# Upper half of the keys from x alone, by weights multiplied on the chip, from the second chunk on

## The reference

```
ct_kv = x @ Wd_kv_w + Wd_kv_b                         # latent, 128 numbers for each token
kt_c  = heads(ct_kv @ Wu_k_w + Wu_k_b)
kt_r  = heads(_rope(x @ Wk_r_w + Wk_r_b, cos, sin))
key   = kt_c + kt_r                                   # 16 heads of 16 numbers
value = heads(ct_kv @ Wu_v_w + Wu_v_b)
```

## Time and profile before

| What | Value |
|---|---|
| Runs | 1925.49, 1926.04, 1926.55 us |
| Profiled execution, its own time | 1926.29 us |
| Its span, first to last instruction | 1924.5 us |
| Mean granted TensorE clock | 0.987 |
| TensorE busy | 1849.6 us (96%) |
| ScalarE busy | 1802.0 us (94%) |
| VectorE busy | 1580.2 us (82%) |
| GpSimd busy | 173.7 us (9%) |
| First exponential of the attention stage | at about 126 us |

### The profile page before, as it was taken

How to read it: one execution, slowest core, us unless ns; L and a number is a source line. 1 busy time by engine, 2 the same in 40 slices (tenths; PEclk the granted TensorE clock), 3 DMA queues, 4 the chain that set the end, 5 groups by cost and what they waited for, 6 DMA issues and landing times.

```text
span 1924.5 us, 31443 instructions
## 1 busy us (share of the span) xinstructions
PE 1849.6 (96%) x12996; PEld 449.9 (23%) x12996; DVE 1580.2 (82%) x1499; ACT 1802.0 (94%) x2022; POOL 173.7 (9%) x132
## 2 busy tenths in 40 slices
PE   8989999999999999999999999999999999999975
PEld 3432222122222222222222222222222222222234
DVE  4858888888888888888888888888889888988467
ACT  3479999999999999999999999999999999999946
POOL 5735400000000000000000000000000000500010
PEclk9989999999999999999999999999999999999987
DMA  4453111111110111111121001111121101111002
GB/s 142 153 172 116 18 21 26 26 26 26 26 26 20 18 18 22 26 26 26 25 70 26 22 17 18 22 26 25 26 48 26 26 19 19 18 23 26 1 24 88
DMA packets 161367, 73.41 MB, mean 38 GB/s; under 512 B 129952, under 2 KB 146592, under 8 KB 160736
## 3 DMA queue, kind: packets, MB, share of 16 engines
q1 hardware_dynamic: 158272, 66.85, 15.0%
q10 hardware_dynamic: 2944, 4.47, 0.8%
HBM read 49.13 MB, written 20.84 MB: 36 GB/s over the span
## 4 chain that ended last, share of the span: by engine, by line
ACT 54%; PE 31%; issue 9%; DVE 4%; DMA 1%; POOL 0%; SPq 0%; ACTq 0%; DVEq 0%; POOLq 0%
ACT arena L901 54%; PE PS L704 15%; PE PS L655 9%; PE PS L1179 4%; PE PS L744 1%; DVE arena L961 1%; PE PS L1328 1%; DMA arena<-tables_dram 1%; DVE bn L832 1%; DVE arena L937 0%; DMA w<-weights_dram 0%; DVE absmax L1771 0%; DVE arena L1805 0%; DVE arena L824 0%; ACT arena L864 0%
## 5 line engine op out<-in xcount | busy, mean ns | idle before, releaser
L901 ACT ACTIVATE arena<-PS 128x1024 f32<-128x1024 f32 x1860 | 1707.8, 1325 | 8.3 <-PE PS L655 5.0
L704 PE MATMUL PS<-arena,Vh 128*32 128x512 f32 x8192 | 1092.6, 606 | 4.1 <-DVE arena L961 4.1
L655 PE MATMUL PS<-Qst,Kst 49*128 49x512 f16 x4096 | 724.0, 384 | 24.5 <-ACT arena L901 4.3
L961 DVE SCALAR_TENSOR_TENSOR arena<-arena 128x2048 f32<-128x2048 f32 x282 | 646.0, 2291 | 0.1
L937 DVE TENSOR_SCALAR arena<-PS 128x512 int32<-128x512 f32 x376 | 259.4, 690 | 247.1 <-PE PS L655 243.3
L655 PEld LDWEIGHTS PS<-Qst,Kst 49*128 49x128 f16 x4096 | 187.7, 93 | 1039.3 <-ACT arena L901 1008.8
L704 PEld LDWEIGHTS PS<-arena,Vh 128*32 128x32 f32 x8192 | 161.3, 108 | 317.5 <-issue 302.5
L957 DVE SCALAR_TENSOR_TENSOR arena<-arena 128x2048 f32<-128x2048 f32 x94 | 216.4, 2302 | 0.0
L945 DVE TENSOR_SCALAR arena<-arena 128x2048 int32<-128x2048 int32 x94 | 116.2, 1236 | 8.5 <-DVE arena L961 0.5
L947 DVE TENSOR_SCALAR arena<-arena 128x2048 int32<-128x2048 int32 x94 | 116.8, 1242 | 0.0
L1496 POOL TENSOR_SCALAR nmr<-mv 128x16 f32<-128x16 f32 x1 | 0.3, 262 | 1256.7 <-DVE mv L1660 1256.7
(11 more groups left out here) (118 smaller groups left out, 480.1 us busy)
## 6 DMA issues: line engine op xcount, KB each, us to landing
Kst<-k_halves SPq DMA_DIRECT2D x64, 128.0 KB
Qst<-q_halves SPq DMA_DIRECT2D x64, 128.0 KB
Vh<-head_values SPq DMA_DIRECT2D x30, 256.0 KB, 5.5
k_halves<-parts_or_sums SPq DMA_DIRECT2D x16, 256.0 KB, 2.9
q_halves<-parts_or_sums SPq DMA_DIRECT2D x16, 256.0 KB, 2.8
Kst<-k_halves SPq DMA_DIRECT2D x64, 64.0 KB
Qst<-q_halves SPq DMA_DIRECT2D x64, 64.0 KB
head_values<-arena SPq DMA_DIRECT2D x1, 4096.0 KB, 16.4
```

The source lines that it names most:

```text
L655: return nc.tensor.matmul(out, Kst[par][low:low + HK + 1, at:at + 128], Qst[par][low:low + HK + 1, j * CH:(j + 1) * CH], start=True, stop= ...
L704: last = nc.tensor.matmul(bank(value_bank(t))[32 * j:32 * j + 32, :], Vh[t % 2][:, kt, :], moving, start=kt == first, stop=kt == last_kt)
L901: nc.scalar.activation(ring(at, k), bank(g % SLOTS * SLOT, k), ACT.Exp, scale=EXP_SCALE).then_inc(a.exp, 1)
L961: last = nc.vector.scalar_tensor_tensor(out=t, in0=t, scalar=POLY[3 - j], in1=power if j == 3 else mantissa, op0=ALU.add, op1=ALU.mult)
```

## The change

It forms the product of the latent weights with the upper key weights once, `Wd_kv_w @ Wu_k_w[:, 128:]`, adds the upper half of `Wk_r_w`, and from chunk 1 on takes the upper keys as two products of x with these weights; the latent bias goes through the same weights into a bias of its own. Chunk 0 stays as it was, three products. The weights lie where the values are written later, and the small products use bank 4, which chunk 1's `KHI` uses next.

TensorE turns the two halves of the latent weights by two transposes ahead of chunk 1's `DKV`, ScalarE copies them to SBUF, and ahead of chunk 1's `DQ_` TensorE makes two products of 128 columns and one of a single column. VectorE adds the rest ahead of its first addition.

```diff
+UPPER_BEFORE = "add", 0, "k"
...
+        latent_t = arena[:, 22 * K1:22 * K1 + D]
+        upper_w = arena[:, 22 * K1 + D:22 * K1 + 2 * D].rearrange("p (k n) -> p k n", k=2)
+        upper_bias = small[:, 0:1]
+        UPPER_BANK = PRODUCT_BANK["p", 1, KHI]
...
-                    KHI: ([wcut(W_KR, k, D, 128) for k in range(2)] + [wcut(W_UK, lo=128)], x2 + [kv]),
+                    KHI: ([upper_w[:, k, :] for k in range(2)], x2) if c else
+                         ([wcut(W_KR, k, D, 128) for k in range(2)] + [wcut(W_UK, lo=128)], x2 + [kv]),
...
-                if e in (UK_, KHI):
+                if e == KHI and c:
+                    pe.wait_ge(s_upper_w, 2)
+                elif e in (UK_, KHI):
                     pe.wait_ge(s_w2, 16)
                     pe.wait_ge(s_ev, DONE["p", c, DKV])
...
+            def turn_latent_weights():
+                pe.wait_ge(s_const, 1)
+                pe.wait_ge(s_ev, DONE[BANK_BEFORE["p", 1, KHI]])
+                for k in range(2):
+                    last = nc.tensor.transpose(PS[:, UPPER_BANK * CH + k * 128:UPPER_BANK * CH + (k + 1) * 128],
+                                               wcut(W_DKV, k, DQ), ident[:, :])
+                last.then_inc(s_upper, 1)
+
+            def upper_weights():
+                pe.wait_ge(s_upper_t, 1)
+                at = UPPER_BANK * CH
+                for k in range(2):
+                    nc.tensor.matmul(PS[:, at + D + k * 128:at + D + (k + 1) * 128], latent_t[:, k * 128:(k + 1) * 128],
+                                     wcut(W_UK, lo=128), start=True, stop=True)
+                nc.tensor.matmul(PS[:, at:at + 1], wcut(W_UK, lo=128), bias[:, B_DKV:B_DKV + 1],
+                                 start=True, stop=True).then_inc(s_upper, 1)
+
             for p in PRODUCTS:
+                if p == ("p", 1, DKV):
+                    turn_latent_weights()
+                if p == ("p", 1, DQ_):
+                    upper_weights()
...
+                if p == ("p", 1, DKV):
+                    act.wait_ge(s_upper, 1)
+                    nc.scalar.copy(latent_t, PS[:, UPPER_BANK * CH:UPPER_BANK * CH + D]).then_inc(s_upper_t, 1)
+                if p == ("p", 1, KHI):
+                    act.wait_ge(s_upper_w, 2)
...
+            def upper_weights():
+
+                dve.wait_ge(s_upper, 2)
+                at = UPPER_BANK * CH
+                past = w[:, W_KR:W_UK].rearrange("p (k n) -> p k n", k=2)[:, :, 128:256]
+                nc.vector.tensor_tensor(upper_w, PS[:, at + D:at + 2 * D].rearrange("p (k n) -> p k n", k=2), past,
+                                        ALU.add).then_inc(s_upper_w, 1)
+                nc.vector.scalar_tensor_tensor(out=upper_bias, in0=PS[:, at:at + 1], scalar=K_SCALE, in1=bias1[:, 0:1],
+                                               op0=ALU.mult, op1=ALU.add).then_inc(s_upper_w, 1)
+
+            dve.wait_ge(s_bias, 2)
             for name, c, n in STEP:
+                if (name, c, n) == UPPER_BEFORE:
+                    upper_weights()
```

More of the change, by code:

```diff
@@ L468, in build @@
         s_swap = {n: [sem(f"{n}_swapped{p}") for p in range(2)] for n in "kq"}
+        s_upper = sem("upper_key_products")
+        s_upper_t = sem("latent_weights_turned")
+        s_upper_w = sem("upper_key_weights_made")
         s_rope = sem("rope_products")
@@ L1365, in evacuate @@
                 at = {DKV: bias[:, B_DKV:B_DKV + 1], DQ_: bias[:, B_DQ:B_DQ + 1], KR_: bias[:, B_KR:B_KR + 1],
-                      UK_: bias[:, B_UK:B_UK + 1], KHI: bias1[:, 0:1], QR_: bias[:, B_QR:B_QR + 1],
+                      UK_: bias[:, B_UK:B_UK + 1], KHI: upper_bias if c else bias1[:, 0:1], QR_: bias[:, B_QR:B_QR + 1],
                       UQ_: bias[:, B_UQ:B_UQ + 1], QHI: bias1[:, 1:2]}[e]
```

## The result

The changed kernel takes 1929.0 us, the median of twenty runs (1926.8 to 1929.9). The kernel before takes 1925.6 on the same chip, also of twenty (1923.8 to 1928.2). The ratio is 1.0016, with a 95% interval of 1.0010 to 1.0023. So the change costs 3.4 us between the medians (3.1 by the ratio, 1.9 to 4.4 by its interval). The forecast was 1929.2, or +3.3 on the profiled execution. The profiled execution of the changed kernel took 1928.93 against 1926.29, and its first exponential of the attention stage starts at 129.43 against 126.28: 3.15 us later, 2.6 us of which are left at the end.

The account below looks back on a forecast made before the run. VectorE and GpSimd taking turns at shared ports were taken to bound the projection stage. 0.8 (late chunk 7 addition) + 3.3 (collision) - 0.8 (slack) gave +3.3 us, about 1929.2 us; range 1925.0 to 1931.2.

Parts of the forecast that it names:

- What bounds the stage: Projection stage: VectorE, full from 39.4 to 76 us through taking turns with GpSimd at shared ports, sets the pace.
- Removed: TensorE, upper key groups from chunk 1 on: seven fp32 products of 512 columns go, saving 6.0 us.
- Added on TensorE: Before chunk 1's first and second groups: eight records of transposes and small products, 1.6 us, bounds 0.9 and 3.4.
- VectorE's added steps and their cover: Before VectorE's first addition: 256-column addition (0.40) and one-column step (0.2), hidden in its wait for GpSimd until 26.23.
- The head shift: Head of VectorE's queue: later turned keys of chunk 1 delay the addition at 39.45 by 0.5 us, ends 0 and 1.7.
- Chunk 7's first addition: VectorE, chunk 7's keys: the addition starts 0.8 us late, from the 0.5 plus what chunk 6's keys add.
- The collision: VectorE's four steps on chunk 7's keys each wait a GpSimd turn of 0.95: 3.8 less 0.5 for pauses, 3.3 us.
- TensorE's lead: TensorE near chunk 7: of 4.3 us of lead, 2.1 remain behind x's load, 3.0 after chunk 7's upper keys.
- The landing: Last table load before the first exponentials: lands 10.66 us after its issue, left unchanged.
- The collision does not form: Rival at chunk 7's keys: swaps land late or VectorE locks first; -1.4 to +1.5 us, middle 1926.3; chance 0.30.
- TensorE sets the end: Rival for the projection stage: VectorE's queue follows TensorE, stage ends 4.3 us early, 1921.8; chance 0.07.
- The head shift passes whole: Rival at VectorE's queue head: shift 1.7 instead of 0.5, plus the collision, 1930.6 to 1931.6; chance 0.15.

Follow-up runs that it names:

- e9: Changed kernel with GpSimd's three turning steps for each part moved to VectorE, ahead of its addition; 1919.82 us against 1926.07 before, ratio 0.9971.
- e10: Kernel before the change with the same move of GpSimd's turning steps to VectorE as e9; 1923.97 us against 1926.07 before, ratio 0.9991.
- e4: Changed kernel with SyncE's last table load issued ahead of the eight loads of the first head's stack; 1927.51 us, ratio to before 1.0011.
- e1: Changed kernel with a third product put back into each upper-key group from chunk 1 on, set-up kept; 1926.49 us, ratio to before 1.0011.
- e3: Changed kernel with GpSimd waiting to begin chunk 6's queries until VectorE has made chunk 7's key low part; 1925.97 us, ratio to before 1.0006.
- e5: Changed kernel with GpSimd held ahead of chunk 6's queries only until VectorE's cast of chunk 7's keys; 1927.79 us, ratio to before 1.0000.
- e6: Changed kernel with e3's wait, last table load between halves of the first head's loads, key lengths and shifts moved into the values; 1926.95 us, ratio 0.9997.
- e8: Changed kernel with e3's wait and the last table load between the two halves of the first head's loads; 1926.89 us, ratio to before 0.9994.
- e2: Kernel before the change with the latent part of the upper keys of chunks 1 to 7 left out, nothing added; 1929.28 us, ratio 1.0021.
- e7: Kernel before the change with all the edits of e6, as its control; 1928.41 us, ratio to before 1.0002.

## Why the prediction was right

The mechanism is the one predicted: the saving closes GpSimd's pause, VectorE's last key steps wait their turns, and the key store holds the reload. That 1929.0 lies so near 1929.2 is luck in part: two terms below came out by errors that cancel.

**What bounds the stage.** Right. VectorE is full from 39.4 us on in both kernels and runs the same 24 instructions. e9 and e10 show it from the other side.

**Removed.** Seven products, 6.0 us: the groups are two records shorter and chunk 7 begins 3.3 us earlier on TensorE.

**Added on TensorE.** Mis-sized. The eight records cost 0.9 us, the lower bound, where I took 1.6 by the weight load of 190 ns. The trace does show 190 ns for each weight load of the small products, but they overlap one another: four take 0.52 us together, and one starts every 0.11 us (21.81, 22.25 after four, 22.47 after two more). That pace is what the records cost. The turned keys of chunk 1 were 0.6 us late by the clock of the trace, and 1.05 against TensorE's own start: in this execution chunk 0's first latent product began at 13.81, before at 14.26.

**VectorE's added steps and their cover.** Right: 0.42 and 0.15, in the idleness that ended at 26.2 before. The second addition now starts at 25.93.

**The head shift.** Too large, though inside its ends of 0 and 1.7. The addition of 39.45 came at 39.16, which is +0.2 if those 0.45 us of an earlier start are taken off. Predicted was +0.5. The sign that I gave, a first addition some 0.5 us later, did not show.

**Chunk 7's first addition.** +0.8 predicted, +0.72 measured (93.45), by other parts than I gave. Chunk 6's addition came 0.44 early (85.70; before 86.14), and from there to chunk 7's two turns more than before were met where I had one: the addition of 85.70 took 1.67 and the cast behind it 1.57, 0.98 and 0.88 more. The sum, -0.44 + 0.98 + 0.88 - 0.62 of idleness used up, is 0.80. A start too early and a turn too many cancel; the agreement is luck.

**The collision.** Right in place and size: the low part's end at 100.13 for 100.15, the reload of the tables at 103.17 for 103.1. This term carries the forecast. One of its parts was wrong: I took four full turns less 0.5 us of pauses between dependent steps. The pauses are as long as before (0.1 us from the addition's end to the cast, in both traces), and the first turn was a half: the four steps are longer by 0.45, 0.88, 0.94 and 1.06, together 3.33 for 3.3. So the addition took 1.14 and not the 1.64 that I had named as a sign.

**TensorE's lead.** Wrong in its cause, and 2.1 us where 3.3 were measured. Gaps were predicted near 78, ahead of chunk 7, for x. The gap came ahead of 74.30, inside chunk 6, for another reason: the latent keys' evacuation stood behind one that waited 3.62 us for VectorE (rows at 72.31 on ScalarE and 74.30 on TensorE). x was there in time. I also had chunk 7's turned keys at 81.8, measured 80.64, and chunk 6's queries at 87.7, measured 86.53; both only fill GpSimd's queue sooner. (The evacuation at 90.68 is that of chunk 6's turned queries, not of the upper ones, as the prediction once calls it.) The 8.2 us gap ahead of 98.07 I hadn't named. It is off the chain in the changed kernel, and e4 shows it is second.

**The landing.** Left at 10.66, measured 11.05: +0.4, which the steps behind it gave back.

**The rivals.** "The collision does not form" would have left 0.69 and 1.22 in those rows; e1 and e3 are what it looks like. "TensorE sets the end" needed a VectorE that isn't held by GpSimd; in e9 and e10 it isn't, and there the gain is 4.2 us. That I gave it 4.3 is luck: my 4.3 holds the mis-sized 1.6 for the set-up, and with the measured 0.9 it would be 5.1. "The head shift passes whole" falls with the 39.16.

Two slips of the pen in the sums change nothing: 96.08 + 4.1 is 100.18, and 1926.04 + 3.3 is 1929.3.

Open: from the first exponential to the last instruction takes 1797.5 to 1800.6 us in these executions, in kernels with the same attention stage. Why it varies by 3 us isn't known. A shift of 1 us or so is blurred by it, so e3, e5, e6 and e8 can't be ranked by their times.

## What to carry to other kernels

Where VectorE and GpSimd are both near full in a stretch, add up VectorE's steps at their lengths when alone, and for each GpSimd step what it holds VectorE up. From 39.4 to 76 us before, VectorE's 24 steps alone would take 6 times 3.29 (0.69, 0.69, 0.69 and 1.22), 19.7 us; the other 16.9 of the 36.6 fall on 18 GpSimd steps, an estimate of 0.94 for each. Where this sum is the bound, work taken from a third engine gains little, and loses where it closes a pause of GpSimd's in which VectorE's last steps on the path ran alone. Look for VectorE durations of two kinds for one shape (0.69 and 1.64), with its reductions from PSUM unchanged. What helped here was to take GpSimd out and not to move its steps in time: a step of 32 rows costs VectorE less to do (0.67) than to be held by (0.94 by that estimate).

## What was not expected of the hardware

- Leaving work out made the kernel slower: 6 us less of TensorE, +0.21% (e2).
- Four fp32 weight loads of 190 ns each fit into 0.52 us, and one starts every 0.11 us. The length of one, as the trace gives it, isn't the pace at which they follow.
- A GpSimd step on 32 rows, 1.25 us when alone, lengthens a VectorE step on 128 rows that it meets in full by 0.88 to 1.07 us.
- The last table load, 128 KB, lands 9.8 to 11.05 us after its issue behind the eight loads of the first head on its queue (before, changed, e1, e2, e3, e5, e9, e10), 5.9 to 7.1 us behind four of them (e6, e7, e8), and 3.1 to 3.3 us ahead of all eight, with the load before it (e4).
